# Two layer norms moved tile by tile into the projections before them, and a first attention's opening in another order

## The chip, the cores and the metric

The kernel runs on one core of one Trainium2 chip. Times are device microseconds of one execution. TensorE (PE) multiplies matrices into PSUM, VectorE (DVE), ScalarE (ACT) and GpSimd (POOL) work on tiles in SBUF, and SyncE (SP) issues every DMA here. Each engine works through a queue of its own, in order, and the queues meet by semaphores.

## The reference

The input x is 16x64x512, that is 1024 tokens of 512, and ctx_4096 is 16 batches of 1601 context rows of 512. Six sublayers follow each other, each on a layer norm of the sum so far:

```python
x = x + _L0_xattn_ref(_layernorm(x, axis=-1), ctx_4096, ctx_4096, Wq, Wk, Wv, Wo)   # 32 query heads of 16, 8 key heads
x = x + _L0_attn_ref(_layernorm(x, axis=-1), A_log, D, x_proj_w, dt_proj_w, dt_proj_b)   # selective scan, width 512
x = x + _L0_ffn_ref(_layernorm(x, axis=-1), ...)      # quantised feed-forward
x = x + _L1_xattn_ref(_layernorm(x, axis=-1), ctx_4096, ...)   # 16 heads of 96
x = x + _L1_attn_ref(_layernorm(x, axis=-1), ...)     # selective scan, width 1024, closes with y @ W_out.T
x = x + _L1_ffn_ref(_layernorm(x, axis=-1), ...)      # base product + softmax-gated low-rank experts
return x
```

The first attention ends with `out @ Wo`. Its softmax runs over the 1601 context rows of a batch.

## The kernel before

X stays in SBUF as eight tiles of 128 tokens by 512. Work is in regions (`Region`), each closed by clearing its semaphores and a barrier of all engines (`restart`, L41), and inside a region in blocks, which also end with a barrier.

**The norm.** `normalised` (L75) is a block of its own: VectorE takes the statistics of all eight tiles, POOL raises the eight variances to the power -1/2 in one operation, VectorE normalises eight tiles, TensorE transposes each into four 128x128 pieces in PSUM, and VectorE and ScalarE copy these to XnT by turns. It is called ahead of five sublayers. The change touches three calls: AN (L1000), BN (L1059) and FN (L2416).

**The opening of the first attention.** The program's first block loads X while POOL makes constants, and SP waits for X (L2557). `l0_attention` (L483) then issues the loads of Wq, Wk, Wv and the first two context chunks and normalises X. Context comes in four chunks of a batch: 512, 384, 384 and 321 columns. The products of K and V need float32 precision, so each operand is split into a high part (a copy to fp32r) and a low part (the rest), and a product is twelve matmuls: four slices by three pairs of parts. `first_batch` (L739) prepares batch 0: VectorE splits Wk and Wv, POOL splits the four context chunks (`split_context`, L630) and then each K (`split_k`, L641), TensorE projects K for four chunks, makes eight query products (a group of heads and a half of the tokens each, L817), projects and transposes V for four chunks, and then makes 16 score tiles (`maximum`, L688), of which VectorE takes the row maxima (`read_maxima`, L667). ScalarE copies the products out (`drain`, L650) and VectorE makes the low part of the queries. SP moves K through memory to stack its parts on partitions (`stack_k`, L615), reloads context (`reload`, L608), and writes the queries and reads them back (`queries`, L566). `all_batches` (L829) is the loop over 16 batches that follows.

**The projection after it.** `project_out` (L402) loads the softmax's reciprocals (`rec`), the attention's outputs and Wo; for each tile TensorE spreads the reciprocals over partitions (`psR`), VectorE multiplies (`on`), TensorE makes the product with Wo, and VectorE adds it to X. Then the weights of the first feed-forward (`FfnWeights`, L1168) and the five small tables of the first scan are loaded, and `l0_mamba` (L1034) normalises X. In its first block (B1, L1065) POOL splits the feed-forward weights (`prepare`).

**The last projection.** The block E4 at the end of `l1_mamba` (L2378) multiplies the scan's output with W_out, 16 matmul records of the trace for a tile, and VectorE adds to X. `l1_ffn` (L2397) issues its five loads, normalises, and goes on.

## Time and profile before

| | us |
|---|---|
| median of 3 runs | 4083.41 (4078.32 to 4084.14) |
| the profiled execution | 4078.03 |
| its span | 4076.2 |
| mean granted clock of TensorE | 0.951 |
| TensorE busy in the span | 3686.4 (90%) |
| VectorE, ScalarE, POOL busy | 2279.4, 1522.8, 1362.2 |
| opening, up to the batch loop | 0 to 115.0 |
| first projection and norm | 1031 to 1097.9 |
| last projection and norm | 3948.8 to 4023.3 |

Times in the rows below count from the span's start. A window's row gives the busy time of each engine with its number of instructions in brackets. In a timeline, like instructions that follow each other are merged, and the bracket at the end names what ended the idle time ahead of them. PEclk is the clock granted to TensorE as a share of the full 2.4 GHz; 0.50 is the low level.

### The profile page before, as it was taken

To read this page: it belongs to the slowest core of one execution; us is meant where nothing else is said; L and a number is where in the kernel's file an instruction comes from. 1 tells how busy PE (TensorE), PEld (TensorE's weight loads), DVE (VectorE), ACT (ScalarE), POOL (GpSimd) and SP (SyncE) were. 2 spreads that over 40 slices of the span, in tenths; PEclk is the share of its full clock that TensorE was granted. 3 is DMA by queue.
4 is the path that set the end of the run, shared out by engine and by line. 5 is a ranking of instruction groups with operands and counts; after the bars stand their busy time and mean duration, and the time that the engine had idled before them with its cause. 6 is when DMAs were issued, how large, how long until landed. Compare 5 with 4: busy or idle time off the path is not lost. (4 is left out here: it accounts for less than half of the span.)

```text
span 4076.2 us, 74868 instructions
## 1 busy us (share of the span) xinstructions
PE 3686.4 (90%) x32200; PEld 2455.6 (60%) x32200; DVE 2279.4 (56%) x2570; ACT 1522.8 (37%) x2188; POOL 1362.2 (33%) x866
## 2 busy tenths in 40 slices
PE   5999999999778599999999999999999988676787
PEld 3555555554333456888878778777777645333334
DVE  3666666665389833444444444444444233787862
ACT  1455555555176312222222222222222111666640
POOL 4344444440189221111111111111111012586871
PEclk9999999998789899999999999999999997797999
DMA  6445555552222032111111111111111210221211
GB/s 187 130 135 148 145 139 137 143 140 51 85 70 75 36 132 62 39 47 39 47 39 47 39 46 31 46 32 44 39 38 40 84 51 3 90 84 52 83 44 39
DMA packets 217969, 301.69 MB, mean 74 GB/s; under 512 B 65520, under 2 KB 163760, under 8 KB 216224
## 3 DMA queue, kind: packets, MB, share of 16 engines
q1 hardware_dynamic: 217640, 296.91, 24.5%
q8 instruction: 255, 4.18, 0.4%
q14 instruction: 74, 0.61, 0.1%
HBM read 243.28 MB, written 53.10 MB: 73 GB/s over the span
## 5 line engine op out<-in xcount | busy, mean ns | idle before, releaser
L1578 POOL TENSOR_TENSOR D_ctx_lo<-D_ctx_raw,D_ctx_hi 128x1904 fp32r<-128x1904 f32 x64 | 255.9, 4000 | 1290.2 <-ACT D_ctx_hi L1572 1290.2
L673 DVE TENSOR_REDUCE A_mxc<-A_psX 128x2 f32<-128x768 f32 (+2 forms) x512 | 485.4, 985 | 208.6 <-PE A_psX L703 207.6
L904 ACT ACTIVATE A_probs<-A_psE 128x1024 f32<-128x1024 f32 (+1 forms) x416 | 426.2, 1025 | 320.5 <-PE A_psE L937 315.4
L1596 ACT ACTIVATE D_V<-D_psY 119x384 f32<-119x384 f32 x224 | 109.8, 490 | 842.9 <-PE D_psY L1663 842.9
L1894 ACT ACTIVATE D_probs<-D_psE 119x2048 f32<-119x2048 f32 x112 | 210.5, 1879 | 414.7 <-PE D_psE L2021 414.7
L1612 DVE TENSOR_REDUCE D_mxc<-D_psE 128x4 f32<-128x1904 f32 (+1 forms) x128 | 242.2, 1892 | 190.6 <-PE D_psE L1682 190.3
L1663 PE MATMUL D_psY<-D_wv_hi,D_ctx_hi 128*119 128x384 f32 (+1 forms) x896 | 314.7, 351 | 16.5 <-DVE D_K_lo L1607 9.0
L1939 DVE TENSOR_TENSOR D_acc<-D_acc,D_probs 119x1024 f32<-119x1024 f32 x96 | 117.6, 1225 | 353.9 <-ACT D_probs L1894 353.9
L2035 PE MATMUL D_psO<-D_probs,D_V 119*32 119x256 f32 (+1 forms) x5376 | 313.3, 381 | 0.0
L1663 PE MATMUL D_psY<-D_wv_hi,D_ctx_lo 128*119 128x384 f32 (+1 forms) x896 | 302.1, 337 | 0.0
L1663 PE MATMUL D_psY<-D_wv_lo,D_ctx_hi 128*119 128x384 f32 (+1 forms) x896 | 301.9, 337 | 0.0
L1653 PE MATMUL D_psY<-D_ctx_hi,D_wk_hi 128*128 128x476 f32 (+1 forms) x768 | 285.8, 372 | 9.8 <-POOL D_ctx_lo L1578 8.2
L1653 PE MATMUL D_psY<-D_ctx_lo,D_wk_hi 128*128 128x476 f32 (+1 forms) x768 | 271.5, 353 | 0.0
L1653 PE MATMUL D_psY<-D_ctx_hi,D_wk_lo 128*128 128x476 f32 (+1 forms) x768 | 269.7, 351 | 0.0
L952 PE MATMUL A_psO<-A_probs,A_V 128*17 128x256 f32 (+1 forms) x3328 | 267.8, 395 | 0.2 <-ACT A_probs L904 0.2
L2035 PEld LDWEIGHTS D_psO<-D_probs,D_V 119*32 119x32 f32 (+1 forms) x5376 | 163.2, 110 | 118.3 <-issue 10.6
L703 PE MATMUL A_psX<-A_Kst,A_Qst 50*128 50x384 f32 (+2 forms) x1024 | 218.5, 424 | 10.7 <-DVE A_mxc L673 6.0
L287 POOL TENSOR_TENSOR ES_hcp<-ES_h_sb,E_Cn 128x512 f32<-128x512 f32 x160 | 203.0, 1279 | 36.2 <-issue 17.9
L639 POOL TENSOR_TENSOR A_ctx_lo<-A_land,A_ctx_hi 128x2048 fp32r<-128x2048 f32 (+1 forms) x64 | 212.6, 3322 | 5.1
L2016 PE MATMUL D_psE<-D_Q_hi,D_K_hi 32*119 32x256 f32 x2688 | 205.5, 293 | 4.7 <-PEq L49 4.7
L2016 PE MATMUL D_psE<-D_Q_hi,D_K_lo 32*119 32x256 f32 x2688 | 195.1, 277 | 0.0
L2016 PE MATMUL D_psE<-D_Q_lo,D_K_hi 32*119 32x256 f32 x2688 | 194.8, 277 | 0.0
(341 smaller groups left out, 7787.4 us busy)
## 6 DMA issues: line engine op xcount, KB each, us to landing
D_ctx_raw<-in_ctx SPq DMA_DIRECT2D x48, 952.0 KB, 5.1
A_land<-in_ctx SPq DMA_DIRECT2D x32, 768.0 KB, 5.5
A_land<-in_ctx SPq DMA_DIRECT2D x16, 1024.0 KB, 5.7
E_Bn<-bc_scratch SPq DMA_DIRECT2D x64, 256.0 KB, 3.6
E_Cn<-bc_scratch SPq DMA_DIRECT2D x64, 256.0 KB, 3.3
k_scratch<-A_Khl SPq DMA_DIRECT2D x32, 384.0 KB, 5.1
A_Kst<-k_scratch SPq DMA_DIRECT2D x64, 192.0 KB, 3.6
A_land<-in_ctx SPq DMA_DIRECT2D x16, 642.0 KB, 4.3
```

Source lines behind the costliest of these rows:

```text
L639: nc.gpsimd.tensor_tensor(lo, land[:, c % 2, :, 0:w], hi.bitcast(F32), ALU.subtract).then_inc(lo_ready, 1)
L673: nc.vector.tensor_reduce(mxc[:, u % 4, :, u // 4], psX[:, x % 2, :, 0:w], axis=AX_X, op=ALU.max).then_inc(x_free, 1)
L703: last = nc.tensor.matmul(psX[:, x % 2, o, 0:w], Qst[b % 2][rows, pair, P * qt:P * qt + P], Kst[b % 2][rows, pair, k0:k0 + w], start=True, ...
L904: nc.scalar.activation(probs[0:KW[k], n % NPR, :, :].rearrange("p h q -> p (h q)"), psE[0:KW[k], :], ACT.Exp, scale=HD ** -0.5).then_inc(e ...
L952: last = nc.tensor.matmul(psO[32 * h:32 * h + HD + 1, 0:HQ], V[j % 2][0:KW[k], k, HG * g + h, :], probs[0:KW[k], n % NPR, 2 * (h % 2) + h ...
L1578: nc.gpsimd.tensor_tensor(ctx_lo[c][:, :, 0:w], ctx_raw[c][:, :, 0:w], ctx_hi[c][:, :, 0:w].bitcast(F32), ALU.subtract).then_inc(lo_done[c ...
L1612: nc.vector.tensor_reduce(mxc[:, H * a:H * a + H, c], psE[:, :, 0:CH[c][1]], axis=AX_X, op=ALU.max).then_inc(x_free, 1)
L1653: last = nc.tensor.matmul(to[:, 0:w], wk_parts[a][:, d, bass.ts(t, P)], parts[a2][:, d, 0:w], start=(n == 0), stop=(n == len(PASSES) - 1))
L1663: last = nc.tensor.matmul(to[0:KWD[k], 0:H * HD], parts[a][:, d, at], wv_parts[a2][:, d, :], start=(n == 0), stop=(n == len(PASSES) - 1))
L1894: nc.scalar.activation(probs[0:KR, N % NPR, :, :].rearrange("p h q -> p (h q)"), psE[0:KR, :, :].rearrange("p h q -> p (h q)"), ACT.Exp, s ...
L2016: nc.tensor.matmul(psE[0:KR, h, bass.ts(i, NQ)], lhs[rows, t, K0[k]:K0[k] + KR], rhs[rows, t, :], start=(t == 0 and lhs is K_parts[0] and ...
L2035: last = nc.tensor.matmul(psO[32 * h:32 * h + 32, t, :], V[0:KWD[k], k, h, bass.ts(t, 32)], probs[0:KWD[k], N % NPR, h, bass.ts(i, NQ)], s ...
```

## The change

There are three parts. A class `TileNorm` does the norm for one tile at a time, with two buffers for the normalised tile. `project_out` and the block E4 use it while their projection still runs: statistics follow each addition, and the transposes of a tile stand in TensorE's queue behind a later tile's product (three tiles later in `project_out`, two in E4). ScalarE alone copies to XnT. The order of the loads around them changes with it: the scan's five tables are now issued before `project_out`, the feed-forward's weights after it, and the last feed-forward's before E4. Norms ahead of the other sublayers are as before.

The opening loads X inside the attention's region, in two halves behind Wk and the first context chunk. ScalarE now makes the high parts of batch 0's context; VectorE makes the low part of chunk 0 and POOL those of the others. The norm is done tile by tile after the first two K chunks, the queries stand between K chunks and are ordered by half of the tokens, and eight of the 16 maxima stand between V chunks.

```diff
+class TileNorm:
+    def statistics(self, dve, t):
+        nc.vector.bn_stats(self.stats[:, t, :], self.X[:, t, :]).then_inc(self.chain, 1)
+        dve.wait_ge(self.chain, 2 * t + 1)
+        nc.vector.bn_aggr(self.mv[:, t, :], self.stats[:, t, :]).then_inc(self.chain, 1)
+        dve.wait_ge(self.chain, 2 * t + 2)
+        nc.vector.tensor_scalar(self.ve[:, t:t + 1], self.mv[:, t, 1:2], EPS, None, ALU.add).then_inc(self.ve_ready, 1)
...
+    def normalise(self, dve, t):
+        dve.wait_ge(self.rstd_ready, t + 1)
+        if t >= 2:
+            dve.wait_ge(self.t_full, t - 1)
+        self.nc.vector.tensor_scalar(self.xn[:, t % 2, :], self.X[:, t, :], self.mv[:, t, 0:1], self.rstd[:, t:t + 1],
+                                     ALU.subtract, ALU.mult).then_inc(self.xn_ready, 1)
+    def transposes(self, pe, t):
+        pe.wait_ge(self.xn_ready, t + 1)
+        for c in range(DC):
+            last = self.nc.tensor.transpose(self.bank(t)[:, P * c:P * c + P], self.xn[:, t % 2, P * c:P * c + P],
+                                            self.consts["ident"][:, :])
+        last.then_inc(self.t_full, 1)
...
 # project_out, VectorE
                     if t >= 2:
                         add(t - 2)
+                    if t >= 3:
+                        norm.normalise(dve, t - 3)
                 for t in range(NPAIR - 2, NPAIR):
                     add(t)
+                    norm.normalise(dve, t - 1)
+                norm.normalise(dve, NPAIR - 1)
 # project_out, TensorE
                     if t + 2 < NPAIR:
                         spread_out(t + 2)
+                    if t >= 3:
+                        transposes(t - 3)
+                for t in range(NPAIR - 3, NPAIR):
+                    transposes(t)
...
 # first_batch, SP
-                        for m in range(NC):
-                            reload(sp, m)
                         for c in range(NC):
+                            reload(sp, c)
                             stack_k(sp, 0, c)
...
 # first_batch, POOL
-                        for c in range(NC):
-                            split_context(pool, link, c)
-                        for c in range(NC):
-                            split_k(pool, link, 0, c)
+                        norm.power_of(pool, range(0, 4))
+                        pool.wait_ge(lo_ready, 1)
+                        rest_of_context(pool, 1)
+                        norm.power_of(pool, range(4, NPAIR))
+                        split_k(pool, link, 0, 0)
+                        for c in range(2, NC):
+                            rest_of_context(pool, c)
+                            split_k(pool, link, 0, c - 1)
+                        split_k(pool, link, 0, NC - 1)
...
 # first_batch, ScalarE
+                        high_of_context(act, 0)
+                        high_of_context(act, 1)
+                        drain(act, ("K", 0, 0))
+                        drain(act, ("K", 0, 1))
+                        for t in range(NPAIR):
+                            norm.out(act, t)
+                        high_of_context(act, 2)
+                        high_queries(0)
+                        high_queries(1)
+                        drain(act, ("K", 0, 2))
+                        high_of_context(act, 3)
...
 # first_batch, VectorE
-                        dve.wait_ge(loaded, 48)
+                        dve.wait_ge(wk_loaded, 16)
+                        split_weights(0, *wkp)
+                        rest_of_context(dve, 0)
+                        for half in range(2):
+                            dve.wait_ge(x_in[half], 16)
+                            norm.statistics_of(dve, range(4 * half, 4 * half + 4))
+                        for t in range(NPAIR):
+                            norm.normalise(dve, t)
+                        dve.wait_ge(wv_loaded, 16)
+                        split_weights(1, *wvp)
...
 # first_batch, TensorE
-                        pe.wait_ge(w_split, 2)
-                        for c in range(NC):
-                            project(pe, ("K", 0, c), range(len(PASSES)))
+                        pe.wait_ge(w_split, 1)
+                        project(pe, ("K", 0, 0), range(len(PASSES)))
+                        project(pe, ("K", 0, 1), range(len(PASSES)))
+                        transposes(0)
+                        transposes(1)
+                        queries_of(0)
+                        queries_of(1)
+                        project(pe, ("K", 0, 2), range(len(PASSES)))
+                        queries_of(2)
+                        queries_of(3)
+                        project(pe, ("K", 0, 3), range(len(PASSES)))
+                        for n in range(G, 2 * G):
+                            queries_of(n)
...
                             project(pe, ("V", 0, c), range(len(PASSES)))
+                            for u in range(max(4 * (c - 2), 0), max(4 * (c - 1), 0)):
+                                maximum(pe, 0, 0, u)
                             project(pe, ("T", 0, c), None)
-                        for u in range(NU):
+                        for u in range(4 * (NC - 2), NU):
                             maximum(pe, 0, 0, u)
...
 # E4, TensorE
                             last.then_inc(full, 1)
+                            if t >= 2:
+                                pe.wait_ge(added, t - 1)
+                                norm.transposes(pe, t - 2)
+                        for t in range(NPAIR - 2, NPAIR):
+                            pe.wait_ge(added, t + 1)
+                            norm.transposes(pe, t)
```

SP's queue in `first_batch`, before (A_land is the landing buffer of context, A_Kst the stacked K, k_scratch the memory it goes through):

```order
L579 DMA A_Kst<-A_ones 2x24x267 [waits A_made,A0_ones_made]
L579 DMA A_Kst<-A_ones 2x24x267
L613 DMA A_land<-in_ctx 128x4x384 [waits A_ctx_split]
L613 DMA A_land<-in_ctx 128x4x321 [waits A_ctx_split]
L613 DMA A_land<-in_ctx 128x4x512 [waits A_ctx_split]
L613 DMA A_land<-in_ctx 128x4x384 [waits A_ctx_split]
L621 DMA k_scratch<-A_Khl 128x2x512 [waits A_k_split]
L627 DMA A_Kst<-k_scratch 32x4x512 [waits A_k_out]
L627 DMA A_Kst<-k_scratch 16x4x512
L627 DMA A_Kst<-k_scratch 32x4x512
L627 DMA A_Kst<-k_scratch 16x4x512
L621 DMA k_scratch<-A_Khl 128x2x384 [waits A_k_split]
```

and after, from the same instruction on:

```order
L666 DMA A_Kst<-A_ones 2x24x267 [waits A_made,A0_ones_made]
L666 DMA A_Kst<-A_ones 2x24x267
L700 DMA A_land<-in_ctx 128x4x384 [waits A_ctx_split]
L708 DMA k_scratch<-A_Khl 128x2x512 [waits A_k_split]
L714 DMA A_Kst<-k_scratch 32x4x512 [waits A_k_out]
L714 DMA A_Kst<-k_scratch 16x4x512
L714 DMA A_Kst<-k_scratch 32x4x512
L714 DMA A_Kst<-k_scratch 16x4x512
L700 DMA A_land<-in_ctx 128x4x321 [waits A_ctx_split]
L708 DMA k_scratch<-A_Khl 128x2x384 [waits A_k_split]
L714 DMA A_Kst<-k_scratch 32x4x384 [waits A_k_out]
L714 DMA A_Kst<-k_scratch 16x4x384
```

The load of the last context chunk of batch 0 (128x4x321) now stands behind the first stack of K rows.

SP's queue from the end of the batch loop, before (A_rec are the reciprocals, A_oT the outputs, CW the feed-forward's weights, B the scan's tables):

```order
L423 UNCONDITIONAL_BRANCH [waits barrier_Pool_Activation_PE_DVE_SP_release]
L425 DMA A_rec<-den_scratch 8x4096
L431 DMA A_oT<-o_scratch 16x4x256 x8
L433 DMA A_wo<-in_L_xattn_Wo 128x4x512
L431 DMA A_oT<-o_scratch 16x4x256 x24
L422 UNCONDITIONAL_BRANCH
L47 ISA [waits barrier_Pool_Activation_PE_DVE_SP_release]
L1189 DMA CW_gu<-in_L_ffn_w_gu 128x2048 [waits barrier_Pool_Activation_PE_DVE_SP_release]
L1189 DMA CW_d<-in_L_ffn_w_down 128x1024
L1189 DMA CW_vec<-in_L_ffn_vec 128x2304
L1058 DMA B_wx<-in_L_attn_x_proj_w 128x192
```

and after:

```order
L47 ISA
L1215 DMA B_wx<-in_L_attn_x_proj_w 128x192 [waits barrier_Pool_Activation_PE_DVE_SP_release]
L1215 DMA B_wdt<-in_L_attn_dt_proj_w 16x512
L1215 DMA B_A<-in_L_attn_A_log 128x64
L1215 DMA B_Dd<-in_L_attn_D 128x4
L1215 DMA B_bias<-in_L_attn_dt_proj_b 128x4
L488 UNCONDITIONAL_BRANCH
L490 DMA A_rec<-den_scratch 8x4096
L496 DMA A_oT<-o_scratch 16x4x256 x8
L498 DMA A_wo<-in_L_xattn_Wo 128x4x512
L496 DMA A_oT<-o_scratch 16x4x256 x24
L487 UNCONDITIONAL_BRANCH
```

The five B loads moved ahead of everything that `project_out` loads, and the CW loads behind it.

TensorE's queue in E4, before:

```order
L2390 MATMUL E_acc<-E_wout,E_U 128x512 [waits A2_w_in]
L2390 MATMUL E_acc<-E_wout,E_U 128x512 x63
L2378 UNCONDITIONAL_BRANCH
L112 UNCONDITIONAL_BRANCH [waits barrier_Pool_Activation_PE_DVE_SP_release]
L117 MATMUL FN_psT<-all_ident,FN_xn 128x128 [waits C_y_full]
L117 MATMUL FN_psT<-all_ident,FN_xn 128x128 x3
```

and after (E_n_xn is the normalised tile):

```order
L2570 MATMUL E_acc<-E_wout,E_U 128x512 [waits A2_w_in]
L2570 MATMUL E_acc<-E_wout,E_U 128x512 x23
L184 MATMUL E_acc<-all_ident,E_n_xn 128x128 [waits C_qiT_out,B_out_done]
L184 MATMUL E_acc<-all_ident,E_n_xn 128x128 x3
L2570 MATMUL E_acc<-E_wout,E_U 128x512 x8
L184 MATMUL E_acc<-all_ident,E_n_xn 128x128 [waits C_qiT_out,B_out_done]
L184 MATMUL E_acc<-all_ident,E_n_xn 128x128 x3
L2570 MATMUL E_acc<-E_wout,E_U 128x512 x8
L184 MATMUL E_acc<-all_ident,E_n_xn 128x128 [waits C_qiT_out,B_out_done]
```

Four transposes now stand behind each product from the third on; before, all stood behind the block's end.

## Rows read from the trace of the kernel before

**Rows 1.** Windows of the opening: us, busy PE PEld DVE ACT POOL, PEclk, DMA share, GB/s.

```profile
12.75:21.75 9.00, 3.20 (x15) 3.20 (x16) 7.19 (x23) 0.60 (x1) 1.66 (x1) 1.00 1.01 365
...
38.10:51.10 13.00, 11.01 (x49) 9.20 (x50) 0.00 (x0) 1.58 (x3) 11.68 (x8) 0.88 0.64 196
51.10:78.20 27.10, 27.10 (x67) 12.03 (x65) 4.84 (x7) 4.62 (x8) 2.82 (x4) 1.00 0.62 150
78.20:95.50 17.30, 12.42 (x65) 9.50 (x63) 0.69 (x1) 4.68 (x9) 10.66 (x4) 1.00 0.88 296
95.50:115.00 19.50, 10.83 (x36) 5.01 (x36) 16.64 (x21) 0.00 (x0) 8.52 (x5) 0.59 0.44 143
```

**Rows 2.** Timeline of the opening: start us, us, engine, line, operation [idle before <-releaser].

```profile
1.69 0.29 POOL L2567 CAST all_identr<-all_ident 128x128 fp32r<-128x128 f32 x1
...
28.14 4.21 POOL L639 TENSOR_TENSOR A_ctx_lo<-A_land,A_ctx_hi 128x2048 fp32r<-128x2048 f32 x1
28.38 4.52 DVE L797 TENSOR_TENSOR A_wklo<-A_VT,A_wkhi 128x512 fp32r<-128x512 f32 x1
...
38.13 0.79 PE L734 MATMUL A_psY<-A_ctx_hi,A_wkhi 128*128 128x512 f32 x1 [13.20 <-DVE A_wvlo L797]
```

**Rows 3.** Timeline from the last projection to the last feed-forward.

```profile
4006.01 0.69 DVE L2383 TENSOR_TENSOR all_X<-E_acc,all_X 128x512 f32<-128x512 f32 x1 [6.18 <-PE E_acc L2390]
...
4015.62 6.35 PE L117 MATMUL FN_psT<-all_ident,FN_xn 128*128 128x128 f32 x32 [9.65 <-DVE FN_xn L99]
...
4022.01 0.60 ACT L125 ACTIVATE F_XnT<-FN_psT 128x512 f32<-128x512 f32 x1 [0.37 <-PE FN_psT L117]
...
4023.26 0.47 PE L2445 MATMUL F_ps<-F_ws,F_XnT 128*128 128x137 f32 x2 [1.29 <-PEq L49]
```

**Rows 4.** Timeline of TensorE from the first projection to the scan's preparation.

```profile
1073.66 7.13 PE L475 MATMUL A_ps<-A_wo,A_on 128*128 128x512 f32 x16
...
1097.88 7.04 PE L1080 MATMUL B_ps<-B_XnT,B_wx 128*48 128x512 f32 x16 [1.27 <-PEq L49]
```

**Rows 5.** Least, median, longest landing of transfers to and from q_scratch, 0 to 120 us.

```profile
DMA to landing us min/median/max: 1.8/4.0/11.3
```

**Rows 6.** Timeline of a tile's norm in the first feed-forward.

```profile
1339.40 0.69 DVE L1242 BATCH_NORM_STATS2 C_stats<-all_X 128x6 f32<-128x512 f32 x1 [0.68 <-PEq L49]
...
1340.34 0.15 DVE L1244 TENSOR_SCALAR C_ve<-C_mv 128x1 f32<-128x1 f32 x1
...
1341.58 0.79 POOL L1324 TENSOR_TENSOR C_rstd<-C_ve,all_minus_half 128x1 f32<-128x1 f32 x1 [0.38 <-DVE C_ve L1244]
```

**Rows 7.** Timeline of the last maximum matmul and of POOL in the block after.

```profile
109.23 0.64 PE L703 MATMUL A_psX<-A_Kst,A_Qst 50*128 50x322 f32 x2 [0.20 <-DVE A_mxc L673]
...
114.99 0.28 POOL L876 MEMSET A_V<- 128x104 f32 x1 [9.10 <-POOLq L49]
```

**Rows 8.** Timeline of SP's queue: a stack of K rows, queries, context loads.

```profile
55.62 0.58 SPq L621 DMA_DIRECT2D k_scratch<-A_Khl  x1
61.07 2.46 SPq L627 DMA_DIRECT2D A_Kst<-k_scratch  x4
...
81.89 3.07 SPq L570 DMA_DIRECT2D A_Qst<-q_scratch  x3
...
90.69 15.78 SPq L613 DMA_DIRECT2D A_land<-in_ctx  x4
```

**Rows 9.** Landing of the context loads of 84 to 112 us.

```profile
DMA to landing us min/median/max: 4.5/5.8/6.5
```

**Rows 10.** Timeline of TensorE in the scan: four transposes.

```profile
1147.72 0.63 PE L370 MATMUL BS_dB<-all_ident,BS_scaled 128*128 128x128 f32 x4
```

**Rows 11.** Timeline of SP: the first and last of the scan's five small loads.

```profile
1083.75 0.62 SPq L1058 DMA_DIRECT2D B_wx<-in_L_attn_x_proj_w  x1
...
1085.89 0.48 SPq L1058 DMA_DIRECT2D B_bias<-in_L_attn_dt_proj_b  x1
```

**Rows 12.** Timeline of VectorE, end of the scan's preparation.

```profile
1130.63 1.23 DVE L1112 SCALAR_TENSOR_TENSOR B_delta<-B_delta,B_du 128x1024 f32<-128x1024 f32 x1 [3.20 <-ACT B_du L1031]
```

More of the change, by code:

```diff
@@ L438, in _ @@
                                       .broadcast_to([heads, heads, hd])).then_inc(sel_made, 1)
+                for t in range(NPAIR):
+                    norm.power(pool, t)
+            @block.scalar
+            def _(act):
+                for t in range(NPAIR):
+                    norm.out(act, t)
             @block.vector
@@ L785, in _ @@
                                                  ).then_inc(hi_out, 1)
+                        high_of_context(act, 0)
+                        high_of_context(act, 1)
+                        drain(act, ("K", 0, 0))
+                        drain(act, ("K", 0, 1))
+                        for t in range(NPAIR):
+                            norm.out(act, t)
+                        high_of_context(act, 2)
[3 more added lines that the diff above has]
+                        high_of_context(act, 3)
+                        high_queries(2)
+                        high_queries(3)
+                        drain(act, ("K", 0, 3))
+                        for n in range(G, 2 * G):
+                            high_queries(n)
                         for c in range(NC):
```

198 lines of the change are left out of this document (141 added, 57 removed).

## The prediction

> **What bounds the kernel now.** I read first the windows that cut the opening into stretches, because the change rebuilds it and one engine's line alone does not show who waits. In [rows 1] TensorE is the engine to follow: it has no K projection before 38.1 us (13.2 us idle before it [rows 2]), then 11.0 us busy of 13.0 (four K chunks), 27.1 of 27.1 (eight query products, so 3.4 us each), 12.4 of 17.3 (V and its transposes), and 10.8 of 19.5 in the maxima, where VectorE has 16.6. So the opening is a late start, then about 58 us in which TensorE runs with short waits, then 19.5 us set by VectorE's reductions. What precedes 38.1 is serial: X's transfer is waited for in the program's first block, the norm follows, and only then are weights and context split. The weight splits are slow by themselves: the subtraction of 128x512 took 4.52 us while POOL's own subtraction of 128x2048 took 4.21 beside it [rows 2]; a VectorE operation on as much data out of PSUM takes 0.69 [rows 3].
>
> Then I read the timelines at the two places where a projection completes X and a norm follows. In both TensorE is busy up to the last tile, and idle or transposing until the next stage: from 1073.66 + 7.13 = 1080.79 to 1097.88, 17.1 us [rows 4]; and from 4005.97 (the addition at 4006.01 follows directly) to 4023.26, 17.3 us [rows 3]. These gaps lie on the path; nothing else runs over them.
>
> **The opening, step by step.** The X transfer no longer closes the first block. The last constant is made at 1.98 [rows 2], a barrier takes some 0.7 (between the last drain's end at 4022.61 and the next block's matmul lie 0.65 [rows 3]), so loads start at 2.7. Seven now stand ahead: Wk 0.26 MB, context chunk 0 1.05, X in two halves 2.10, chunk 1 0.79, Wq 1.05, Wv 0.26. At 365 GB/s [rows 1], with 1.8 us as the least time to landing [rows 5], chunk 0 is in at 9.5, X at 15, chunk 1 at 17.4, the rest by 21.
> Chunk 0: ScalarE's copy of 2048 columns at four times 0.60 at most [rows 3], take 2.1; VectorE's subtraction at most four times 0.69, take 2.5: ready at 14.1. K chunk 0 takes 4.4 us on a slow clock and ends at 18.5. Chunk 1 (three quarters as wide): copy 1.7 to 19.1, POOL's subtraction 3/4 of 4.21 [rows 2] to 22.3. VectorE does statistics of X in that time (0.69 for a tile [rows 6]); they hide. Then TensorE has work without a hole: K chunk 1 3.2, eight tiles of transposes at 6.35/8 = 0.79 [rows 3] to 31.9, two queries to 38.7, K chunk 2 3.0, two queries to 48.5, K chunk 3 2.9, four queries to 65.0. The covers for this: context chunk 2 is split by POOL after ScalarE's eight drains, at 37.6, 1.1 us before TensorE wants it; chunk 3 is loaded only after the first stack of K rows (SP waits in order), is ready at about 46.8, 1.7 before it is wanted. If either cover goes, the wait is that many microseconds.
> So V starts at 65.0 instead of 78.2: 13.2 earlier. Of 16 maxima, eight now stand between V chunks. Four cost TensorE some 3.2 us, two VectorE reductions' wait, and hide a drain of 1.1: V and these eight take 21.5, to 86.5. The other eight at 0.9 (14.4 us from 95.5 to 109.87 for 16 [rows 1, 7]) end at 93.8; the tail from the last maximum at 109.87 to the next block at 114.99 is 5.1 [rows 7]. TensorE's side would end at 98.9, 16.1 earlier.
> A second chain ends later. SP does its K stacks in order, each from issue to last issue 61.07 + 2.46 - 55.62 = 7.9 us [rows 8]. The third cannot start before 48.8, so the fourth ends at 63.4; the first queries are written (+2.6, landing 1.8 [rows 5]) and read back in eight issues at 1.02 [rows 8], to 72.5 to 74.8. They land at 75 to 77, and the first maximum wants them at 77: a tie. Behind them SP writes the other queries, which took 11.3 us to land [rows 5], and the loads of context for batch 1 queue behind these: landed at 86 to 88. POOL then splits two chunks, 4.6 + 3.9 us, to about 96; the last load (5.8 to land [rows 9]) is waited for by SP before the block ends: about 101.5. I take this chain, as the later: **13.5 us**, with 16.1 as the one end, and 8 as the other if both covers and the tie go wrong.
>
> **The first projection (attention to scan).** Removed is the 17.1 us gap. Instead the last tile has a chain of its own: addition 0.69, statistics to variance 1340.34 + 0.15 - 1339.40 = 1.09, the power on POOL 0.79 [rows 6], normalising at most 0.69, transposes 0.63 on a fast clock [rows 10], drain 0.60, next block 0.65, and 0.3 of semaphores: 5.4. The other tiles' norms lie beside TensorE: VectorE has some 3.5 us of work in a tile's period of about 5 (7.13 us for the products of two tiles [rows 4], and the spreading between them). Four tiles' transposes now precede the last product, 4 x 0.63 = 2.5, all on the path. And five small loads stand ahead of the reciprocals, outputs and Wo in SP's queue, from 1083.75 to 1085.89 + 0.48 = 2.6 us [rows 11] that used to lie beside the norm; TensorE waits for Wo, so they are paid. 17.1 - 5.4 - 2.5 - 2.6 = **6.6**, bounds 3 (transposes at 0.79, larger delay of the loads) and 9 (loads hidden).
> The feed-forward weights are now loaded after the norm, so POOL's 17.5 us of splitting starts some 8 us later in the next block, beside VectorE's operations with two SBUF inputs. In [rows 2] such a pair took as long as POOL's. The rule for it is the Trainium skill's, SBUF — State Buffer, "Who interferes with whom": a VectorE instruction with two SBUF inputs and a GpSimd one that reads SBUF exclude each other for the whole instruction. The trace of the weight split agrees (4.52 beside 4.21). By the rule about four operations of 1.2 us become 3.5, and what POOL's end and the 3.20 us that VectorE idles there [rows 12] don't take up is under 1 us; without the rule the cost is zero. I take zero, 0 to 1.
>
> **The last projection (scan to last feed-forward).** Five tiles of transposes precede the last product, 5 x 0.63 = 3.2; the five weight loads now stand before the projection and are long in. 17.3 - 5.4 - 3.2 = **8.7**, bounds 6.5 and 10.
>
> **Sum.** 13.5 + 6.6 + 8.7 = 28.8. The profiled execution took 4078.03, so 4049.2 by its own time; the median of the runs shown is 4083.41, which gives 4054.6. I predict 4054.
>
> **Rivals.**
> - *SP's queue sets the opening.* Every stack of K rows and the chunk 3 load wait for each other in order; if queries land 5 us after 77, both chains slip by 5. For it: 7.9 us a stack, and the tie. Against: nothing else is in that queue. Opening 8.5, total 23.8, 4059.6.
> - *VectorE and POOL hold each other up.* In the opening, normalising beside POOL's subtraction, +3, and 1 in the scan's preparation: total 24.8, 4058.6. Against: K chunk 1 waits for that same subtraction, so most is covered. This is the rule named above taken at its worst.
> - *Slower: TensorE's clock stays at 1.2 GHz in the opening.* The new order has a hole between K chunks 0 and 1, and short waits later. On the low level the queries cost 27.1 more, K 5, V 9: 41 us against 28.8 gained, 4095.7. It decides from about 70% of that stretch at the low level. Against: after 13.2 us without any matmul [rows 2] the stretch from 38.1 has 0.88 granted and the next 1.00 [rows 1], so about 3 us were slow. A page states the mechanism: the Trainium skill, TensorE: Matmul & The Clock Gate, "What's actually happening", says that the low level is the default and activity lifts it. The trace agrees, and I have priced K chunk 0 and the transposes on the low level for it.
> - *No change.* The stages after wait for something else (a load, a barrier), and the shortened tails go into that wait. Against: the next blocks' loads are all issued before the norm. 4083.
>
> **How the numbers follow.** Forecast 0.65, SP's queue 0.15, the mutual hold 0.12, slower 0.03, no change 0.05. Adding the lower ends, 8 + 3 + 6.5 = 17.5, gives 4066; the upper, 16.1 + 9 + 10 = 35, gives 4048; the medians themselves move by a few microseconds (4078.32 to 4084.14 before), so the range is 4043 to 4069, and both milder rivals lie in it. 0.2% is 8.2 us, about what a measurement of this kernel tells from none. Only the last two cases reach inside it: faster 0.93, same 0.04, slower 0.03.
>
> **What would show it.** The batch loop's first memset on POOL near 101.5 instead of 114.99, TensorE with no hole over 2 us from 22 to 77, V from about 65. The reduction that opens maxima waiting for TensorE and not TensorE for the query rows. 5 to 6 us from the last product to the next block at both later places, and the first product there about 2.6 us later after the attention. It is wrong if queries arrive after V chunk 2 is done, if chunk 3's load is late, or if a granted clock under 0.8 stands anywhere between 31 and 80 us.

## Result and the profile after

The changed kernel took 4057.97 us in the median of five runs (4052.99 to 4061.63), the kernel before 4082.07 beside it (4078.32 to 4084.14): ratio 0.9943, 95% interval 0.993 to 0.9955, so 23 us faster, give or take 5. The profiled execution took 4052.99 against 4078.03, 25.0 us less. The forecast was 4054, with a range of 4043 to 4069 (4049.2 by the profiled time): a gain of 28.8 us, where the two medians lie 24.1 apart. Three single executions among the experiments (4277.5 and 6063.23 us with the context loads ahead, 6989.17 with the opening alone) were disturbed and stand in no median or ratio here.

I first put the trace of the changed kernel beside the marks the prediction had named. The opening in windows, the first four of the five stretches of [rows 1] (columns as there):

```profile
12.75:21.75 9.00, 4.41 (x12) 3.23 (x12) 8.78 (x19) 1.97 (x2) 3.88 (x2) 0.90 1.03 369
38.10:51.10 13.00, 13.00 (x47) 7.97 (x46) 2.07 (x3) 3.89 (x6) 5.70 (x6) 1.00 0.62 188
51.10:78.20 27.10, 22.84 (x82) 13.05 (x81) 6.13 (x7) 5.06 (x9) 10.88 (x5) 1.00 0.61 197
78.20:95.50 17.30, 11.72 (x40) 7.06 (x40) 12.87 (x17) 1.42 (x3) 8.51 (x4) 0.50 0.64 223
```

TensorE works from 13.5 us on and is full through the second window (13.00 of 13.00; before 11.01). The same timeline as [rows 2] and [rows 7], for the marks of the opening:

```profile
6.26 0.69 DVE L914 TENSOR_TENSOR A_wklo<-A_VT,A_wkhi 128x512 fp32r<-128x512 f32 x1
13.47 0.76 PE L821 MATMUL A_psY<-A_ctx_hi,A_wkhi 128*128 128x512 f32 x1 [13.47 <-DVE A_ctx_lo L834]
...
62.55 0.79 PE L821 MATMUL A_psY<-A_ctx_hi,A_wvhi 128*128 128x512 f32 x1
...
74.30 0.73 PE L790 MATMUL A_psX<-A_Kst,A_Qst 50*128 50x512 f32 x4
...
92.42 0.64 PE L790 MATMUL A_psX<-A_Kst,A_Qst 50*128 50x322 f32 x2 [0.20 <-DVE A_mxc L760]
...
96.64 1.40 DVE L771 CAST A_Qst<-A_psX 2x512 fp32r<-2x512 f32 x2 [1.27 <-PE A_psX L799]
...
101.45 0.28 POOL L1028 MEMSET A_V<- 128x104 f32 x1 [6.32 <-POOLq L49]
```

V starts at 62.55 (forecast 65.0, before 78.16), the first maximum waits for nothing but the product ahead of it, the last one is over at 93.06 (93.8), and the batch loop's first memset stands at 101.45 (101.5; before 114.99): 13.54 us gained. VectorE's copy of the row of maxima ends at 98.04; the block closes 3.4 us after that. Who is late is in SyncE's queue, the rows that answer to [rows 8]:

```profile
55.02 0.62 SPq L708 DMA_DIRECT2D k_scratch<-A_Khl  x1
61.81 2.48 SPq L714 DMA_DIRECT2D A_Kst<-k_scratch  x4
...
72.44 23.27 SPq L700 DMA_DIRECT2D A_land<-in_ctx  x4
```

The four context loads are issued over 23.3 us, the last at 95.7, and SyncE waits for it to land. What SyncE waits for at the end of the block (us in total, times, longest):

```profile
SPq L862 <- DMA A_land<-in_ctx: 4.2, 1, 4.2
```

The load lands at 99.94 and the block ends 1.5 us behind that. It ends 1.4 to 1.5 us behind this landing in all five traces that have this opening unchanged.

The first projection, answering to [rows 4] and [rows 11]: SyncE's first and last small load, the first product and what it waits for, the last products, the last tile's power and drain, the scan's first products.

```profile
1016.58 0.35 SPq L1215 DMA_DIRECT2D B_wx<-in_L_attn_x_proj_w  x1
...
1018.39 0.43 SPq L1215 DMA_DIRECT2D B_bias<-in_L_attn_dt_proj_b  x1
...
1031.16 6.65 PE L558 MATMUL A_ps<-A_wo,A_on 128*128 128x512 f32 x8 [4.26 <-DMA A_wo<-in_L_xattn_Wo]
...
1067.34 3.60 PE L558 MATMUL A_ps<-A_wo,A_on 128*128 128x512 f32 x8
...
1072.88 0.80 POOL L171 TENSOR_TENSOR A_n_rstd<-A_n_ve,all_minus_half 128x1 f32<-128x1 f32 x1 [3.08 <-DVE A_n_ve L148]
...
1075.30 0.60 ACT L190 ACTIVATE B_XnT<-A_psT 128x512 f32<-128x512 f32 x1 [0.62 <-PE A_psT L184]
...
1076.54 9.50 PE L1238 MATMUL B_ps<-B_XnT,B_wx 128*48 128x512 f32 x16 [1.27 <-PEq L49]
```

From the last product's end, 1070.94, to the next block are 5.6 us (before 17.1). The last projection, answering to [rows 3]:

```profile
3983.10 7.03 PE L2570 MATMUL E_acc<-E_wout,E_U 128*128 128x512 f32 x16
...
3993.61 1.09 PE L184 MATMUL E_acc<-all_ident,E_n_xn 128*128 128x128 f32 x4 [0.30 <-DVE E_n_xn L178]
...
3996.00 9.64 PE L2633 MATMUL F_ps<-F_ws,F_XnT 128*128 128x137 f32 x64 [1.30 <-PEq L49]
```

5.9 us from 3990.13 to 3996.00 (before 17.3).

The account, from marks in both traces (start of the batch loop, its last attention product, the scan's first product, the scan's own block, the last projection, the router's first product, the router's second group, the store of the result):

| stretch | before, us | after, us | difference |
|---|---|---|---|
| to the batch loop | 114.99 | 101.45 | -13.54 |
| batch loop | 910.32 | 909.26 | -1.06 |
| first projection | 72.57 | 65.83 | -6.74 |
| scan's preparation | 37.01 | 40.42 | +3.41 |
| scan to last projection | 2813.94 | 2813.57 | -0.37 |
| last projection | 74.43 | 65.47 | -8.96 |
| router's first products | 7.60 | 9.48 | +1.88 |
| rest | 37.92 | 38.25 | +0.33 |

The three terms of the forecast came out as 13.5, 6.7 and 9.0. What it did not have are the two stretches that got longer, 5.3 us, and both begin with TensorE's first products behind a shortened tail (the stretch between a projection's last product and the next block): 9.50 us where [rows 4] have 7.04, 9.64 where the kernel before took 7.76.

### The profile page after: what moved, and what is told of

Its sections match the earlier page's. It is cut to its first block and busy times, and to the rows that moved or that the text cites. A ratio compares the mean times of both kernels' runs of the same rounds, so it can differ in the third digit from the quotient of the medians.

```text
span 4051.2 us, 74876 instructions
## 1 busy us (share of the span) xinstructions
PE 3688.3 (91%) x32200; PEld 2454.3 (61%) x32200; DVE 2272.4 (56%) x2574; ACT 1535.5 (38%) x2204; POOL 1361.9 (34%) x876
## 5 line engine op out<-in xcount | busy, mean ns | idle before, releaser
L726 POOL TENSOR_TENSOR A_ctx_lo<-A_land,A_ctx_hi 128x1536 fp32r<-128x1536 f32 (+2 forms) x60 | 199.2, 3321 | 4.8
```

## The experiments

The theory: each of the three terms stands by itself; SyncE's queue sets the opening; and TensorE now comes out of the tail with a low granted clock. Rivals: the loss in the preparation is VectorE and POOL holding each other up (the forecast had priced that at nothing), or comes with the opening; the opening's end is set by VectorE's maxima. Experiments are told by what they change against the changed kernel.

**The opening alone; the late norms alone.** First the new `first_batch` with the old `project_out`, scan, last projection and `normalised`, then the reverse.

> The new opening alone; the projection after the first attention, the last projection and the norms behind them are those of the kernel before. If the terms of the prediction stand by themselves, the opening's block ends at 101.5 us as in the changed kernel (before 115.0) and the profiled time is 13.5 to 14.6 us below the 4078.0 of before, 4063.4 to 4064.5; the first projection's last product lies 17.1 us ahead of the scan's first product again, that product group takes 7.0 us (changed kernel 9.5), and the router's takes 7.8 (9.6). Rival, that part of the 3.1 us lost in the scan's preparation comes from the opening (other start time, other state of the loads): the scan's first products take about 9.5 us here too, and the time is about 4066.5.

Measured: 4067.03 profiled and in the median, ratio 0.997 (0.9958 to 0.9981). The scan's first products took 7.04 and the router's 7.76, with 16.9 and 16.2 us behind the last products again. The time is 2.5 to 3.6 us above the one expected, because the opening ended at 103.24 and not at 101.5. It lies near the rival's 4066.5, but without the rival's cause: that asked for first products of 9.5 us.

> The two late projections with the norm tile by tile; the opening is that of the kernel before. Sum by the changed kernel's trace: first projection -6.75, scan's preparation +3.1, last projection -8.96, router's first products +1.9, in all -10.7: 4067.3 by the profiled time of before, 4078.0. The granted clock in the 9.5 us behind the scan's first product is about 0.74 (before 1.00), and the router's 64 products take about 9.6 us (before 7.8). Rival, that the 3.1 and 1.9 us are not of these edits: both product groups at 7.0 and 7.8 us, and 4062.3.

Measured: 4066.70 profiled, 4067.05 in the median, ratio 0.9969 (0.9957 to 0.9981). Batch loop at 115.16; products of 8.72 and 10.11 us behind the tails. The time is 0.6 us from the expected 4067.3. So the parts add up: ratios 0.997 and 0.9969 give 0.9939 together, measured 0.9943, and the lengthened products belong to the late norms.

**Context loads ahead of the queries' writes** (the theory that SyncE's queue ends the opening).

```
+    if b.start:
+        reload(sp, NC)
+        reload(sp, NC + 1)
     for part, ready in ((0, hi_out), (1, lo_out)): ...
-    for m in range(NC, 2 * NC):
+    for m in range(NC + 2, 2 * NC):
```

> The changed kernel, with SyncE's queue of the opening in another order: the loads of batch 1's third and fourth context chunks stand ahead of the two large writes of the remaining queries, not behind them. If SyncE's wait for the last context load sets the end of the opening (101.45 with POOL idle 6.3 us before it), POOL's splits end by about 86 to 88 instead of 95.1, the last load has landed by 96, and the block ends with TensorE's and VectorE's chain at 98.0 plus some 0.5: 98.5 to 98.9, 2.6 to 2.9 us earlier, 4050.3 by the profiled time. VectorE's CAST of mpz beside POOL's subtraction (0.98 us) may fall to about 0.2, 0.8 more. Rival, that the wait is for bytes and not for their order (3.8 MB of writes at 350 GB/s, 11 us, now end last): the block ends at 101 to 102 again, 4053. Second rival: the earlier loads slow the queries' stacks, the first maximum waits, and nothing is gained.

Measured: 4053.04 profiled, 4052.87 in the median, ratio 0.9933 (0.9921 to 0.9946). The timeline of SyncE, POOL and VectorE at the opening's end:

```profile
74.26 3.46 SPq L700 DMA_DIRECT2D A_land<-in_ctx  x2
83.75 5.26 SPq L700 DMA_DIRECT2D A_land<-in_ctx  x2
...
85.76 2.68 POOL L726 TENSOR_TENSOR A_ctx_lo<-A_land,A_ctx_hi 128x1284 fp32r<-128x1284 f32 x1
99.65 0.28 POOL L1031 MEMSET A_V<- 128x104 f32 x1 [11.21 <-POOLq L49]
...
95.36 0.17 DVE L765 CAST A_mpz<-A_nm 128x8 fp32r<-128x8 f32 x1
97.01 1.40 DVE L771 CAST A_Qst<-A_psX 2x512 fp32r<-2x512 f32 x2 [1.27 <-PE A_psX L799]
```

POOL is done at 88.4 instead of 95.1, the loads are issued by 89.0 instead of 95.7, the copy of mpz takes 0.17 without POOL beside it (0.98 in the changed kernel), and the block closes 1.2 us behind VectorE's last copy, not 3.4. The mechanism is as expected; the gain in the opening is 1.8 us and not 2.6 to 2.9. V began only 0.25 us later than in the changed kernel (62.80), but the first maximum 1.25 later (75.55), and TensorE stood for 0.96 us before it: the third stack of K rows had taken 10.1 us instead of 7.6, so the last read of the first queries was issued by 74.2 instead of 71.4. The opening with SyncE's old order ended at 101.45, 103.24, 102.93, 104.35 and 105.75 us in five traces; with the new order at 99.65, 97.22 and 100.70 in three. By these means, 103.5 against 99.2, the order is worth some 4 us; the ratios of the two kernels (0.9933 and 0.9943) point the same way, but their intervals overlap. In the trace that ends at 100.70 (all changes together with Wo's load ahead, the last experiment) SyncE again stood for 10.2 us before the last context load, and the block closed 2.4 us behind VectorE's copy. So the first rival, that bytes and not their order end the block, has a part there.

**Unread products in the tails.** TensorE multiplies into a bank that nobody reads, in time in which it waits.

```
+    transposes(NPAIR - 3); busy(2, 512)
+    transposes(NPAIR - 2); busy(1, 128)
+    transposes(NPAIR - 1); busy(1, 256)
```

> The changed kernel, with TensorE given products whose results nobody reads in the tails of the two late projections: behind the last product two of 512 columns (four in the last projection), one small one between the last two tiles' transposes and one or two behind them, all in time in which it waits there. If the low granted clock of the next block's first products comes from TensorE's idle stretches in the tail (2.4 busy of 5.6 us), the scan's first products take 7.0 us in place of 9.5, VectorE's first delta stands 9.8 us behind the first product in place of 12.6, the router's 64 products 7.8 in place of 9.6: 2.8 + 1.9 = 4.7 us, 4048.3 by the profiled time. Rival, that the clock falls by itself there (time since the last long stretch, or the light products of the scan's preparation themselves) or that the loss is VectorE's and POOL's port: the same 9.5 and 9.6 us, and 4053.0, or up to 1 us more for fillers that run late.

Measured: 4053.76 profiled, 4055.07 in the median, ratio 0.994 (0.9928 to 0.9952); the opening ended 1.48 later than in the changed kernel. Windows of the tail and the next products in both projections, changed kernel first (columns as in [rows 1]):

```profile
1070.94:1076.50 5.56, 2.36 (x16) 1.54 (x14) 2.75 (x6) 2.28 (x4) 0.80 (x1) 0.84 0.00 0
1076.50:1086.00 9.50, 9.46 (x16) 2.36 (x16) 0.68 (x1) 0.51 (x2) 0.00 (x0) 0.74 0.79 291
3990.10:3996.00 5.90, 2.25 (x14) 1.40 (x12) 2.75 (x6) 1.79 (x3) 0.82 (x2) 0.75 0.00 0
3996.00:4005.50 9.50, 9.50 (x65) 9.50 (x66) 0.00 (x0) 0.00 (x0) 8.84 (x1) 0.80 0.00 0
```

```profile
1072.80:1078.40 5.60, 4.71 (x25) 2.83 (x23) 2.74 (x6) 2.28 (x4) 0.80 (x1) 1.00 0.00 0
1078.40:1088.00 9.60, 8.75 (x20) 2.73 (x21) 1.37 (x2) 0.51 (x2) 0.00 (x0) 1.00 0.80 301
3992.00:3998.50 6.50, 5.97 (x26) 3.45 (x24) 2.70 (x6) 1.79 (x3) 0.80 (x1) 1.00 0.00 0
3998.50:4008.00 9.50, 9.38 (x69) 8.45 (x70) 1.06 (x5) 0.26 (x1) 8.87 (x1) 1.00 0.01 2
```

With TensorE busy 4.7 of 5.6 us and 6.0 of 6.5 the granted clock stays at 1.00 and the products take 7.04 and 7.76. The whole does not show the gain: by the ratio (0.994 against 0.9943) the kernel with unread products is no faster, and its opening was the later one. The first delta stands 9.83 behind the first product (12.63 in the changed kernel). Four products of 512 columns were too many in the last projection: they took 3.60 us and made the tail some 0.8 longer. The forecast gain was 4.7; of this the preparation kept 2.0 (38.44 us instead of 40.42), since VectorE now was late there: the rival had a part in it.

How often the clock falls: behind the last projection's tail without unread products in all eight traces that have it (9.56 to 10.11 us), behind the first projection's in six of eight (8.72 to 9.54; 7.04 in two); with unread products (three traces) or with the 32 transposes of before (two) never. Little work does not always lower it: with the context loads ahead TensorE was busy 2.2 of 5.4 us in the first projection's tail and kept 1.00, and the products took 7.04. Nor did the gap of before keep the clock up by itself. In its first stretch TensorE does nothing, in the second it makes most of the 32 transposes, the third leads up to the scan's first product:

```profile
1080.80:1090.00 9.20, 0.00 (x0) 0.00 (x0) 6.72 (x20) 0.00 (x0) 1.65 (x1) 0.76 0.66 249
1090.00:1096.00 6.00, 5.87 (x28) 5.88 (x29) 5.15 (x11) 1.65 (x3) 0.00 (x0) 0.51 0.31 108
1096.00:1097.88 1.88, 0.61 (x6) 0.40 (x5) 0.69 (x1) 0.76 (x3) 0.02 (x1) 1.00 0.00 0
```

The clock had fallen there too; the transposes ran on it (0.51 granted) and it was back at 1.00 before the products that count. The change took that stretch of work away together with the wait.

**The small loads behind the projection's; then the feed-forward weights too.**

```
     for n in range(TOK // QT): ...      # SyncE in project_out
+    behind()                            # wx, wdt, A, D, bias
```

> The changed kernel, with the five small loads of the scan's constants issued behind the first projection's own loads, not ahead of them. If their 2.3 us on SyncE's queue are what puts the first Wo product late, it starts 17.8 us behind the start of the last attention product, as before the change (changed kernel 20.45, 19.7 to 21.0 in the runs so far), and the time is 2.6 us under the changed kernel's 4053.0: 4050.4. Rival, that the product waits for the reciprocals' round trip and the bytes of the values: 20 us again, 4053.

Measured: 4053.61 profiled, 4054.13 in the median, ratio 0.9938 (0.9924 to 0.9951). The first Wo product stands 17.73 behind the last attention product (17.83 before the change, 20.45 after): 2.7 us from these two traces. Over all traces it is 19.69 to 21.03, mean 20.2, in the seven with the small loads ahead, and 17.65 to 18.61, mean 17.9, in the six without: 2.3 us, and the five issues take 2.2 in the changed kernel (1016.58 to 1018.82). The opening ended at 104.35 here, 2.9 later than in the changed kernel, so the time does not show it.

> As the run before, and the three loads of the feed-forward weights also stand behind the projection's loads, so that GpSimd's preparation starts with the scan's block and not some 11 us into it. If VectorE and GpSimd held each other at the end of the scan's preparation (VectorE's last copy ended 5.4 us behind ScalarE's last softplus in the context-ahead run, 3.65 before the change), the stretch from the scan's first product to its next block falls to 37.0 us (39.3 with the clock high, 40.4 in the changed kernel), GpSimd ends its splits before VectorE's first update of delta, and each of VectorE's 128x1024 updates takes 1.2 us. Time 4053.0 - 2.6 - 2.3 to 3.4 = 4047.0 to 4048.1. Rivals: the clock alone made the loss (40.4 stays where the first products take 9.5 us, and the time is 4050.4), or the 3 MB of weights hold up the projection's values and cost up to 8 us ahead of the first product.

Measured: 4051.61 profiled, 4054.06 in the median, ratio 0.9935 (0.9923 to 0.9948), with the opening's end at 105.75. Here the preparation took 39.32 and not the 37.0 expected, with first products of 8.73 (1.7 lost to the clock). The two engines in the preparation's end, first with the late weights and the clock high (the context-ahead run), then with the early ones:

```profile
1095.97 3.26 DVE L1276 TENSOR_TENSOR B_du<-B_delta,B_XnT 128x1024 f32<-128x1024 f32 x1
1099.62 2.91 DVE L1273 SCALAR_TENSOR_TENSOR B_delta<-B_delta,B_du 128x1024 f32<-128x1024 f32 x1
...
1094.94 3.21 POOL L1367 TENSOR_TENSOR CW_gu_lo<-CW_gu,CW_gu_hi 128x1024 fp32r<-128x1024 f32 x1
1098.11 3.34 POOL L1365 TENSOR_TENSOR CW_d<-CW_d,CW_vec 128x1024 f32<-128x1024 f32 x1
```

```profile
1097.96 1.23 DVE L1276 TENSOR_TENSOR B_du<-B_delta,B_XnT 128x1024 f32<-128x1024 f32 x1
1099.57 1.22 DVE L1273 SCALAR_TENSOR_TENSOR B_delta<-B_delta,B_du 128x1024 f32<-128x1024 f32 x1
...
1091.46 2.35 POOL L1367 TENSOR_TENSOR CW_d_lo<-CW_d,CW_d_hi 128x1024 fp32r<-128x1024 f32 x1
```

VectorE's multiplication of two SBUF operands takes 3.26 beside POOL's and 1.23 alone; its last copy ends 5.4 us behind ScalarE's last softplus there, 3.65 here as before the change. So the pair costs up to 1.7 us. With the clock high in both, the preparation takes 37.62 and 37.64 us with the early weights (the two runs of everything together) and 38.44 to 40.04 with the late ones (three traces). The changed kernel's own trace hides this cost: its clock was low, ScalarE came later, and VectorE had caught up.

**All maxima behind V.**

```
-    for u in range(max(4 * (c - 2), 0), max(4 * (c - 1), 0)):
-        maximum(pe, 0, 0, u)
     project(pe, ("T", 0, c), None)
- for u in range(4 * (NC - 2), NU):
+ for u in range(NU):
```

> The changed kernel, with all 16 maxima of batch 0 behind the V projections; in the changed kernel eight stand between them. TensorE then has V and its transposes done by about 80 instead of 86.5, and sixteen maxima at VectorE's pace (1.16 and 0.89 each, some 15.3 us in all) end at about 96.5 instead of 93.1, the row of maxima at 101.4 instead of 98.0. If SyncE's wait sets the block's end (101.5 to 103.2 in the runs of this opening), the end does not move by more than 0.5 and the time is 4053 to 4054. Rival, that VectorE's chain sets it: the end comes 3.4 us later, 4056.4.

Measured: 4058.07 profiled, 4055.16 in the median, ratio 0.9943 (0.993 to 0.9955), as the changed kernel. The block ended at 100.43, VectorE's copy at 98.41, only 0.4 us later than in the changed kernel (3.4 expected): the sixteen reductions took 14.7 us. So the interleaving of maxima bought next to nothing on VectorE's side either, and this run does not tell whether SyncE would cover a larger loss there.

**What the order of loads is worth; what the interleaving of keys and queries is worth.** First Wq and Wv ahead of Wk, context and X; then all four K projections ahead of transposes and queries.

> The changed kernel, with Wq and Wv loaded ahead of Wk, context and X in the opening, in the order of the kernel before; each still has a semaphore of its own. Wq is 1.05 MB and Wv 0.26 MB, at the 365 GB/s of this stretch 3.6 us. If the place of these loads is what the prediction's opening rests on, the first key product starts at 17.1 to 18.3 in place of 13.5 to 14.7, everything up to the queries follows by 3.6, and the block ends 3 to 4 us later than in the runs with this opening (100.4 to 105.8), near 106.5. Rival, that SyncE's slow issues of the two (2.3 and 3.0 us in the changed kernel, when its queue is full) cost the same wherever they stand: the third chunk is then loaded no later, the K stacks follow each other at SyncE's 8 us as before, and the block ends within 1 us of the others.

Measured: 4059.78 profiled, 4059.18 in the median, ratio 0.995 (0.9937 to 0.9964). The first product stands at 16.91, V at 65.59, 3.0 later than in the changed kernel and as expected from the bytes. The block's end at 106.45 is 5.0 later than in the changed kernel's trace and 2.9 later than the mean of the five with the opening unchanged, 103.5. By the ratios (0.995 against 0.9943) the whole is 2.9 us slower, but their intervals overlap.

> The changed kernel, with all four key projections ahead of the transposes and the queries, on TensorE and ScalarE; the order of loads is kept. TensorE then waits for the third chunk's parts from 26.2 to about 31.6, K2 and K3 run from 31.6 to 38.7, transposes and queries to about 69.5, and V starts there in place of 62.6. The K stacks are done early, SyncE's queue writes the remaining queries at 70 as now, so TensorE sets the end: 98.0 + 7 = 105, the block at 105.5, 2.5 us over the mean of the runs with this opening; 4055 to 4057. Rival, that SyncE's K stacks (8 us each) and what is behind them set the end whatever TensorE does: the block ends at 101 or under, since they now end 8 us earlier, and the time falls to 4051.

Measured: 4069.64 profiled, 4067.75 in the median, ratio 0.997 (0.9958 to 0.9981). Both theories were far too mild:

```profile
30.61 0.66 PE L821 MATMUL A_psY<-A_ctx_hi,A_wkhi 128*128 128x384 f32 x1 [5.29 <-POOL A_ctx_lo L834]
41.85 0.61 PE L821 MATMUL A_psY<-A_ctx_hi,A_wkhi 128*128 128x322 f32 x1 [7.51 <-POOL A_ctx_lo L834]
...
78.42 0.80 PE L821 MATMUL A_psY<-A_ctx_hi,A_wvhi 128*128 128x512 f32 x1
...
113.28 0.28 POOL L1020 MEMSET A_V<- 128x104 f32 x1 [11.21 <-POOLq L49]
```

TensorE stood 5.3 and 7.5 us before the third and fourth chunk, V began at 78.4 instead of 62.6, and the block ended at 113.28, 11.8 later. The fourth chunk's load is queued on SyncE behind the first K stack in either order (issued at 30.8 in both), and its parts were ready at 41.7; this second wait the expectation did not have. The two products behind the waits also ran on a low clock (0.60 granted from 30.6 to 34.4, 0.50 from 41.8 to 45.2). In the changed kernel transposes and four queries lie in that time. From these single traces 11.8 of the opening's 13.5 us hang on this interleaving; against the mean of five, 103.5, it is 9.8 of 11.5, and by the ratios (0.997 against 0.9943) 11 us.

**Together.** Context loads ahead, all late loads behind the projection's, unread products in both tails; then Wo's load ahead of the values' as well.

> Three changes on the changed kernel: context loads ahead of the queries' writes in the opening, all late loads behind the first projection's own, and unread products in both tails (two of 512 columns in the last projection now, since four ran 0.85 us past the tail). By the parts: opening -1.8, first product -2.6, scan's preparation -3.1, router's first products -1.9, in all -9.4: 4043.6 by the profiled time. Rival, that the parts overlap (the opening's gain is lost at the first projection, or the loads of the weights disturb it): 4047 or above.

Measured: 4047.85 profiled, 4046.81 in the median, ratio 0.992 (0.9908 to 0.9933). Opening 97.22, first Wo product 17.68 behind, the preparation 37.62, the last tail and the router's products 5.4 and 7.76: every part did its work. Yet the time is 4.2 us above the expected 4043.6, and 3.4 of that are the batch loop, 912.71 against 909.26 in the changed kernel. In the thirteen traces, which share its code, it took 908.8 to 912.7. Cut at its 32 reciprocals, the 28 stretches in the middle of the loop are the same in all of them (800.4 to 800.8 us together). The difference lies at its two ends and goes with the granted clock: 36.7 to 39.2 us at the start with 0.94 to 0.87 granted, 19.9 to 24.2 in a stretch of TensorE's work at the end. That stretch in the changed kernel, here, and in the next run:

```profile
967.28:987.77 20.49, 16.13 (x162) 7.63 (x162) 13.98 (x19) 11.59 (x13) 0.00 (x0) 0.92 0.00 1
962.50:986.65 24.15, 22.02 (x160) 10.37 (x162) 13.92 (x19) 11.62 (x13) 0.00 (x0) 0.59 0.00 1
966.33:986.23 19.90, 15.23 (x160) 7.17 (x162) 14.01 (x20) 11.59 (x13) 0.00 (x0) 0.98 0.00 1
```

What decides the clock there from one execution to the next stays open. What the opening gains is seen in the whole only with that much blur.

> The three changes together, and Wo's load in the first projection ahead of the values' eight small ones. TensorE waited 3.6 us for Wo there, 17.7 us from the start of the last attention product to the first Wo product. Wo issued 5 us earlier has landed by then, and the product waits for the first values alone, whose issues move back by 0.6: about 15.0 us, 2.7 us earlier, 4044.1 by the median of the three together (4046.8). Rival, that the values' landing or the reciprocals set it within 1 us: 17 us, and no difference.

Measured: 4046.75 profiled, 4045.90 in the median, ratio 0.9916 (0.9903 to 0.993). The rival held:

```profile
1026.37 1.29 DVE L523 TENSOR_TENSOR A_on<-A_oT,A_psR 128x512 f32<-128x512 f32 x2 [13.54 <-DMA A_oT<-o_scratch]
1027.21 3.75 PE L558 MATMUL A_ps<-A_wo,A_on 128*128 128x512 f32 x4 [4.12 <-DVE A_on L523]
```

The first product waits for VectorE's `on`, and that for the values from `o_scratch`: 17.67 us again. Wo was merely the later of two.

## Why the prediction was right

- *The opening, 13.5.* Right in cause: SyncE's chain ended it, 3.4 us behind TensorE's side (forecast 98.9 against 101.5; measured 98.0 against 101.45), and context loads put ahead of the writes brought the block's end within 1.2 us of VectorE's. That the size is exact is in part luck. The profiled execution is the fastest of its five, and its opening the earliest of the five traces that have it unchanged; by their mean, 103.5, the gain is 11.5. Details cancelled as well. V started 2.5 us earlier than forecast (the queries 0.9 shorter in sum, the transposes 5.6 and not 6.35, K chunks 2 and 3 together 1.2 shorter), but V and the first eight maxima then took 24.0 and not 21.5.
- *The clock in the opening.* It was granted in full up to 78 us and at 0.50 from there on. The forecast had called itself wrong if less than 0.8 stood anywhere before 80, so that sign came out, two microseconds inside. In this trace it cost nothing, since SyncE ended the block later anyway.
- *Both rivals of the opening.* The tie went right in this trace: the queries landed in time, and the first maximum at 74.30 did not wait for them. It went wrong in five of the nine traces with this order of maxima, where TensorE stood 0.7 to 1.7 us before the first maximum. The mutual hold of VectorE and POOL did occur: the copy of mpz took 0.98 us in the changed kernel (0.17 alone) and 2.2 to 2.7 in four others, ahead of an end that SyncE set. The measured 4057.97 is nearest to that rival's 4058.6, but not for its reason; the loss sat behind the tails.
- *First projection, 6.6.* Measured 6.7, with 5.6 for the tail (5.4), 2.6 for the small loads as forecast (2.3 by the means of the traces) and 2.1 left for what the sum had as four tiles' transposes (2.5).
- *Last projection, 8.7.* Measured 9.0, with 5.9 for the tail (5.4) and so 2.5 for the five tiles' transposes (3.2).
- *The step that was missed.* The tails were taken out with what follows unchanged. The forecast watched the clock in the opening alone and gave it nothing behind the tails. There TensorE is at work 2.2 to 2.4 us of 5.6 to 5.9, and the first products behind it ran partly on the low level of 1.2 GHz: 2.8 us up to VectorE's first delta in the preparation and 1.9 in the router. Unread products in that time removed both. The total stayed in the range because this is small beside it, and because the three terms came out. The Trainium skill, TensorE: Matmul & The Clock Gate, "What's actually happening", cited in the forecast, has the low level as the default and activity as what lifts it. The traces agree: with 4.7 us busy of 5.6 the granted clock was 1.00, with 2.4 of 5.6 it was 0.84 in the tail and 0.74 behind it.
- *The port, 0 to 1.* Mis-sized. The forecast applied the rule of the Trainium skill, SBUF — State Buffer, "Who interferes with whom", and estimated 3.5 us for an operation that takes 1.2 alone; measured 3.26, as the rule has it. But the cost at the end of the preparation is up to 1.7 and not under 1 once the clock is high. In the profiled run it lay behind ScalarE.
- *Sums of the forecast that do not follow from their own terms.* Context chunk 0: 2.7, 1.31 MB at 365 GB/s and 1.8 make 8.1, not 9.5 (its copy started at 9.08). The fourth stack of K rows, 48.8 and twice 7.9, ends at 64.6, not 63.4 (measured 64.28). The query reads, 63.4 + 2.6 + 1.8 and eight at 1.02, end at 76.0, not at 72.5 to 74.8; measured, the eight were issued in 4.0 us, by 71.4. So that the queries were there in time also rests on reads twice as fast as priced.

Open stays 0.6 us in the change of blocks ahead of the scan: from VectorE's last copy to POOL's first instruction are 0.63 us in the kernel before and with the late norms alone, 0.96 with the opening alone, and 1.25 with both, in every trace. So it does not come with the late norms by themselves; no run here isolates the cause.

## What to carry to other kernels

When a norm is taken off the path tile by tile, what is left between two dense stretches of TensorE is a few microseconds of light work. In this kernel the next stage's first products paid for that with a low clock in most executions: read the granted clock of the next stage, and try unread products on TensorE, sized to the wait. The five small loads that lost their hidden place were paid in full, 2.3 us: put them behind the loads the next stage waits for. Where one engine issues loads, round trips and stores in order, the block can end with that queue, as it did here; then a new order of work on the other engines pays where it fills a wait that the queue makes (queries between K chunks, 10 to 12 us) and not where it does not (maxima between V chunks). And one trace is not enough for a term of a few microseconds: the same opening ended over a range of 4.3 us.

## What was not expected of the hardware

- The granted clock fell behind a light tail in most executions, not in all: 0.74, 0.82 or 1.00 in the same 9.5 us of the same code.
- VectorE's operations on 128x8 elements can take as long as POOL's that runs: a TENSOR_TENSOR of mpz took 2.52 us, a CAST 0.98 and 2.22, alone 0.17; the longest such CAST took 2.67.
- The same opening ended anywhere from 101.45 to 105.75 us. SyncE's stack of the third chunk, from its write's issue to its last read's, took 7.6 us in the changed kernel and 10.1 with the context loads ahead, with the same bytes and nothing changed up to there. In the five traces with the opening unchanged it took 7.6, 8.5, 10.2, 10.8 and 10.9 us, where the block ended at 101.45, 102.93, 103.24, 104.35 and 105.75: the longer the stack, the later the end.
- The same work of the batch loop's end took 19.9 to 24.2 us in thirteen traces, with 0.98 to 0.59 of the clock granted, while its middle stayed within 0.4 us.
